# One core, attention block between two feed-forward halves: the last batch put first, head 0 staged from small writes, value groups moved behind

## The reference

```python
x = x + 0.5 * ffn(layernorm(x))          # layernorm again inside, 512 hidden, ternary weights, gelu, layernorm
x = x + attention(layernorm(x))
x = x + 0.5 * ffn(layernorm(x))
# attention, 16 heads of 8 channels
q = heads(x @ Wq + bq); k = heads(x @ Wk + bk); val = heads(x @ Wv + bv)
pos = (sinusoid(512, 128) @ Wp + bp) per head
score = (einsum(q + u, k) + relative_shift(einsum(q + v, pos))) / sqrt(8)
out = einsum(softmax(score), val) @ Wo + bo
```

## Time and profile before

| | |
|---|---|
| median of three runs | 447.42 us (446.59 to 447.7) |
| the profiled execution's own time | 447.46 us |
| its span, first to last instruction | 445.3 us |
| DVE busy over the span | 398.2 us (89%) |
| PE busy | 357.0 us (80%) |
| ACT busy | 263.9 us (59%) |
| POOL busy | 113.4 us (25%) |
| mean granted TensorE clock | 0.959 of full speed |

### The profile page before, as it was taken

How to read it: one execution, slowest core, us unless ns; L and a number is a source line. 1 busy time by engine, 2 the same in 40 slices (tenths; PEclk the granted TensorE clock), 3 DMA queues, 4 the chain that set the end, 5 groups by cost and what they waited for, 6 DMA issues and landing times.

```text
span 445.3 us, 18049 instructions
## 1 busy us (share of the span) xinstructions
PE 357.0 (80%) x7328; PEld 288.1 (65%) x7328; DVE 398.2 (89%) x579; ACT 263.9 (59%) x650; POOL 113.4 (25%) x157
## 2 busy tenths in 40 slices
PE   1869898756979889898898987988989889676974
PEld 1647675645767767677676766776767767573664
DVE  8786988429999999999999999999999999948685
ACT  1666555316666666666666666666666666614980
POOL 7543745390020201202102022020120210025552
PEclk9988899969899999999999999999999999988898
DMA  7005147920322313213133132231321301500002
GB/s 213 1 1 186 51 148 245 296 62 12 81 57 43 81 26 87 68 31 84 40 65 75 19 88 56 44 80 20 88 64 30 89 7 25 75 18 2 0 26 71
DMA packets 60182, 30.67 MB, mean 69 GB/s; under 512 B 36880, under 2 KB 58928, under 8 KB 60016
## 3 DMA queue, kind: packets, MB, share of 16 engines
q1 hardware_dynamic: 59376, 29.22, 25.8%
q10 hardware_dynamic: 576, 0.73, 0.6%
q0 software_dynamic: 192, 0.18, 0.2%
HBM read 19.11 MB, written 11.01 MB: 68 GB/s over the span
## 4 chain that ended last, share of the span: by engine, by line
DVE 58%; issue 17%; PE 11%; ACT 5%; POOL 2%; SPq 2%; DMA 2%; DVEq 1%; POOLq 0%; ACTq 0%
DVE pT L894 30%; DVE negmax L886 19%; PE pair L1014 3%; ACT v_rep L602 2%; DVE xh L702 2%; ACT v_rep L590 1%; PE pair L969 1%; DVE v_rep L820 1%; DVE sqsum L814 1%; DMA qs_scratch<-pT 1%; SPq L309 1%; PE pair L1183 1%; DMA stage_k<-kc_scratch 1%; DVE stat L692 1%; PE pair L1116 1%
## 5 line engine op out<-in xcount | busy, mean ns | idle before, releaser
L633 ACT ACTIVATE probs<-pair,negmax 128x512 f32<-128x512 f32 x256 | 173.7, 683 | 111.3 <-DVE negmax L886 111.3
L886 DVE TENSOR_REDUCE negmax<-pair 128x2 f32<-128x1024 f32 x128 | 152.1, 1188 | 10.4 <-PE pair L1133 10.4
L894 DVE STREAM_TRANSPOSE pT<-probs 128x1024 f32<-128x1024 f32 x128 | 157.0, 1226 | 0.5 <-ACT probs L633 0.5
L1116 PE MATMUL pair<-stage_k,stage_c 128*32 128x512 f16 x1024 | 117.2, 408 | 47.4 <-ACT probs L633 40.8
L1122 PE MATMUL pair<-stage_z,stage_q 128*32 128x512 f16 x1024 | 111.4, 384 | 0.0
L1133 PE MATMUL pair<-stage_z,stage_q 128*32 128x438 f16 (+58 forms) x1024 | 102.9, 282 | 0.0
L508 POOL COPY v_diag<-v_rep 32x512 f32 (+1 forms) x64 | 38.9, 607 | 233.9 <-PE pair L1148 226.5
L1128 PE MATMUL pair<-stage_z,stage_q 128*32 128x16 f16 (+50 forms) x1024 | 97.9, 277 | 0.0
L1148 PE MATMUL pair<-pT,v_diag 128*32 128x128 f32 (+1 forms) x2176 | 93.3, 271 | 3.6 <-DVE pT L894 3.6
L1116 PEld LDWEIGHTS pair<-stage_k,stage_c 128*32 128x32 f16 x1024 | 50.7, 140 | 69.5 <-ACT probs L633 55.4
L1148 PEld LDWEIGHTS pair<-pT,v_diag 128*32 128x32 f32 x2176 | 73.3, 114 | 4.1 <-DVE pT L894 3.8
(11 more groups left out here) (112 smaller groups left out, 326.0 us busy)
## 6 DMA issues: line engine op xcount, KB each, us to landing
stage_z<-z_scratch SPq DMA_DIRECT2D x16, 254.0 KB
qs_scratch<-pT SPq DMA_DIRECT2D x12, 256.0 KB, 2.7
stage_q<-qs_scratch SPq DMA_DIRECT2D x126, 24.0 KB
stage_z<-z_scratch SPq DMA_DIRECT2D x16, 128.0 KB
qc_scratch<-pT SPq DMA_DIRECT2D x8, 256.0 KB, 3.5
kc_scratch<-pT SPq DMA_DIRECT2D x8, 256.0 KB, 3.5
stage_k<-kc_scratch SPq DMA_DIRECT2D x16, 128.0 KB
stage_z<-z_scratch SPq DMA_DIRECT2D x16, 127.5 KB
```

The source lines that it names most:

```text
L633: nc.scalar.activation(probs[:, q % 6, :], score_pair(q // 2)[:, q % 2, :], ACT.Exp, bias=negmax[:, q % 8:q % 8 + 1], accum_out=rowsum[:, ...
L886: nc.vector.tensor_reduce(negmax[:, 2 * n % 8:2 * n % 8 + 2], score_pair(n)[:, :, :], AX.X, ALU.max, negate=True).then_inc(max_ready, 1)
L894: nc.vector.transpose(pT[:, par, 2 * n:2 * n + 2, :].rearrange("p a s -> p (a s)"), probs[:, 2 * n % 6:2 * n % 6 + 2, :].rearrange("p a s ...
L1116: mm(bank[32 * j:32 * j + 32, :], all_rows[:, 32 * j:32 * j + 32], stage_k[:, par, :], start=True, stop=False, skip_group_check=True)
```

## The change

Five things are edited.

1. **Order.** The last batch's moments move from step 20 to 18 and its statistics from 21 to 19, its tiles from 22 to 21, its turn from 23 to 22. The products of batch 2 move from step 22 to 23, directly ahead of batch 3's. The rounding of a batch's products stands ahead of the copy of `xT` in a step.
2. **Value groups.** No group goes with the first three batches. Twelve follow the last products on PE, and four (12 to 15) stand inside head 0, behind its score tiles 8, 10, 12 and 14. ACT copies those four behind the exponentials of tiles 9, 11, 13 and 15. ACT copies twelve of the 16 groups, DVE four.
3. **Writes.** Batch 3's data for head 0 go out in small writes: the first 16 channels of its queries (one DMA on SP, two on ACT), the first 8 of its content queries (two on SP). The rest of batch 3 and the keys of batch 2 are written by SP when head 0's own loads have landed (nine DMAs). Scratch layouts change so that a head's rows lie together.
4. **Head 0's loads.** Keys go from SBUF to SBUF without DRAM (`first_keys`, two DMAs a batch: on POOL for batches 0 to 2, on SP for batch 3). The eight query reads are split four and four between SP and POOL.
5. **Head 1's loads.** The eight query reads of head 1 move from SP to POOL, where they stand behind the spreading of head 0's values. PE waits for them with `staged_second`.

```diff
+MOMENT_STEPS = ({8: 0, 12: 1, 16: 2, 18: 3}, {8: 0, 12: 1, 16: 2, 20: 3})
+X_STEPS = ({9: 0, 13: 1, 17: 2, 19: 3}, {9: 0, 13: 1, 17: 2, 21: 3})
+XHAT1_STEPS = {12: 0, 16: 1, 20: 2, 21: 3}
+TURN1_STEPS = {14: 0, 18: 1, 21: 2, 22: 3}
+QK_STEPS = {17: 0, 20: 1, 23: 2, 24: 3}
...
-V_EARLY = 6
-LOADS_FIRST = 6
+V_HEAD = 12
+V_DVE = (5, 7, 9, 11)
+V_ACT = tuple(m for m in range(V_GROUPS) if m not in V_DVE)
+V_TILES = {8: 12, 10: 13, 12: 14, 14: 15}
...
+        def first_keys(eng, b, done):
+
+            c = slice(b * S, (b + 1) * S)
+            for a in range(2):
+                r = 32 * b + 16 * a
+                eng.dma_start(stage_k[r:r + 16, 0, :], rep_ap(half[0:HP, 2 + a, c], [(0, 2), (1, S)]))\
+                    .then_inc(done, 16)
...
# SP
+            sp.wait_ge(v_extended, 2 * B)
+            write_queries(sp, B - 1, 0, slice(0, EARLY), q_first)
+            sp.wait_ge(q_split, 2 * B)
+            write_content(sp, B - 1, 0, 1, u_first)
+            sp.wait_ge(k_split_last, 1)
+            first_keys(sp, B - 1, staged[0])
+            sp.wait_ge(q_out, 16 * 3 * (B - 1))
+            sp.wait_ge(q_first, 16 * 3)
             sp.wait_ge(stage_zero, 8)
-            stage_queries(sp, 0, 0, staged[0], range(NI - 2))
-            sp.wait_ge(k_out, 32 * B)
-            stage_keys(sp, 0, 0, staged[0])
+            stage_queries(sp, 0, 0, staged[0], range(4))
+            sp.wait_ge(u_first, 32)
+            stage_content(sp, 0, 0, B - 1, staged[0])
+
+            sp.wait_ge(staged[0], 16 * LOADS_EVEN)
+            sp.wait_ge(k_split, B - 1)
+            write_keys(sp, B - 2)
+            for kind in range(3):
+                write_queries(sp, B - 1, kind, slice(EARLY, D), q_out)
+            write_content(sp, B - 1, 1, H, u_out[B - 1])
+            write_keys(sp, B - 1)
 
             for b in range(B):
                 sp.wait_ge(u_out[b], 32)
                 stage_content(sp, 1, 1, b, staged[1])
+            sp.wait_ge(k_out, 32 * B)
             stage_keys(sp, 1, 1, staged[1])
-            stage_queries(sp, 1, 1, staged[1])
...
# POOL, behind ffn(0)
-            stage_queries(pool, 0, 0, staged_first, range(NI - 2, NI))
-            pool.wait_ge(u_out[B - 1], 32)
-            stage_content(pool, 0, 0, B - 1, staged_first)
+            pool.wait_ge(q_out, 16 * 3 * (B - 1))
+            pool.wait_ge(q_first, 16 * 3)
+            stage_queries(pool, 0, 0, staged_pool, range(4, NI))
...
             for par in range(2):
-                pool.wait_ge(v_copied[par], V_GROUPS // 2)
+                pool.wait_ge(v_copied[par], len((V_ACT, V_DVE)[par]))
             spread_v(0, 0)
+            pool.wait_ge(q_out, 16 * 3 * B)
+            stage_queries(pool, 1, 1, staged_second)
             spread_v(1, 1)
...
# ACT, in ffn(0) behind the rounding of batch 3, and in head 0
+                        if QK_STEPS[n - 1] == B - 1:
+                            act.wait_ge(q_high, 2 * B - 1)
+                            write_queries(act, B - 1, 1, slice(0, EARLY), q_first)
+                            act.wait_ge(v_extended, 2 * B - 1)
+                            write_queries(act, B - 1, 2, slice(0, EARLY), q_first)
...
+            for q in range(NQ):
+                exp_tile(0, q)
+                if q - 1 in V_TILES:
+                    copy_values(V_TILES[q - 1])
...
# PE
+                if m in (0, 2):
+
+                    pe.wait_ge(q_split, m + 4)
+                    pe.wait_ge(k_split, m // 2 + 2)
+                elif m >= 4:
+                    values_copied(pe, m - 2 if m >= V_HEAD else m - 4)
...
+                    if first and q in V_TILES:
+                        v_product(V_TILES[q])
...
-            pe.wait_ge(staged_first, 16 * LOADS_FIRST)
-            head(0, 0, 16 * (LOADS - LOADS_FIRST), True)
-            head(1, 1, 16 * LOADS)
+            pe.wait_ge(staged_pool, 16 * LOADS_POOL)
+            head(0, 0, 16 * LOADS_EVEN, True)
+            pe.wait_ge(staged_second, 16 * NI)
+            head(1, 1, 16 * LOADS_ODD)
```

More of the change, by code:

```diff
@@ L111, in macaron_kernel @@
         pTf = pT[:, :, :, :].rearrange("p a q s -> p (a q s)")
-        wq_sb, wk_sb, wv_sb, wp_sb = (pTf[:, 128 * n:128 * n + 128] for n in range(4))
+        wq_sb, wk_sb, wp_sb = (pTf[:, 128 * n:128 * n + 128] for n in (0, 1, 3))
+        wv_sb = wv[:, :]
         embT = pTf[:, 512:1024]
@@ L254, in v_bank, with values_copied @@
         def v_bank(n):
-            return 2 + n % 2 if n < V_EARLY else 2 + (n - V_EARLY) % 4
+            return 4 + n % 2 if n >= V_HEAD else 2 + n % 4
         def v_groups(step):
[L260 to L263, removed]
+            return range(V_HEAD) if QK_STEPS.get(step) == B - 1 else ()
+        def values_copied(eng, m):
+            by_dve = m in V_DVE
+            eng.wait_ge(v_copied[by_dve], (V_ACT, V_DVE)[by_dve].index(m) + 1)
         def score_pair(n):
@@ L309, in stage_queries, with write_queries, write_content, write_keys @@
                 eng.dma_start(dst, src).then_inc(done, 16)
+        def write_queries(eng, b, kind, r, done):
+            rows = (rep_ap(vl[r, b, :], [(NG, 2), (1, S)]), rep_ap(vh[r, b, :], [(0, 2), (1, S)]),
+                    rep_ap(vh[r, b, NG:], [(0, 2), (1, S)]))[kind]
+            eng.dma_start(qs_dram[r, :, kind, b * S:(b + 1) * S], rows).then_inc(done, 16)
+        def write_content(eng, b, h0, h1, done):
+            c = slice(b * S, (b + 1) * S)
+            for a in range(2):
+                eng.dma_start(qc_dram[h0:h1, b, a].rearrange("h p d n -> h (p d n)"), half[HP * h0:HP * h1, 0:2, c])\
+                    .then_inc(done, 16)
+        def write_keys(eng, b):
+            c = slice(b * S, (b + 1) * S)
+            for a in range(2):
+                eng.dma_start(kc_dram[:, b, a].rearrange("h p d n -> h (p d n)"),
+                              rep_ap(half[:, 2 + a, c], [(0, 2), (1, S)])).then_inc(k_out, 16)
         def rep_ap(view, dims):
@@ L338, in _ @@
             stage_pos(1, 1)
[L340 to L344, removed]
+            for b in range(B - 1):
+                sp.wait_ge(q_high, 2 * b + 1)
+                write_queries(sp, b, 1, slice(0, D), q_out)
+                sp.wait_ge(v_extended, 2 * b + 1)
+                write_queries(sp, b, 2, slice(0, D), q_out)
@@ L353, in _ @@
-                if b < B - 1:
+                write_content(sp, b, 0, H, u_out[b])
+                if b < B - 2:
                     sp.wait_ge(k_split, b + 1)
[L355 to L360, removed]
-            sp.wait_ge(stage_zero, 8)
@@ L465, in ffn @@
                             .then_inc(s["x_const"], 1)
-                    g = (n - 8) // 4
-                    if n % 4 == 0 and 0 <= g < B:
+                    g = MOMENT_STEPS[f].get(n)
+                    if g is not None:
                         r, v = grs[:, 4 * g:4 * g + 4], gvar[:, 4 * g:4 * g + 4]
@@ L642, in take_o @@
                 nc.scalar.activation(o_sb[:, par, :], ps[4 + par][:, 0:128], ACT.Copy).then_inc(o_ready, 1)
-            for h in range(2):
-                for q in range(NQ):
-                    exp_tile(h, q)
+            for q in range(NQ):
+                exp_tile(0, q)
+                if q - 1 in V_TILES:
+                    copy_values(V_TILES[q - 1])
+            for q in range(NQ):
+                exp_tile(1, q)
             for h in range(2, 4):
@@ L822, in ffn @@
                         nc.vector.tensor_tensor(sq_low, sqsum[:, :], sq_high, ALU.subtract).then_inc(s["sq_split"], 1)
-                    g = (n - 9) // 4
-                    if n % 4 == 1 and 0 <= g < B:
+                    g = X_STEPS[f].get(n)
+                    if g is not None:
                         dve.wait_ge(s["grstd"], g + 1)
@@ L876, in _ @@
             nc.vector.tensor_tensor(bo_row, bo_row, ps[6][:, 0:D], ALU.add).then_inc(bo_ready, 1)
-            for b in range(B):
-                dve.wait_ge(u_out[b], 32)
-            dve.wait_ge(k_out, 32 * B)
-            dve.wait_ge(q_out, 16 * 3 * B)
             def row_max(h, n):
@@ L891, in turn @@
                 dve.wait_ge(probs_ready, h * NQ + (2 * n + 2))
+                if n == 0 and isinstance(h, int) and h == 1:
+                    for b in range(B):
+                        dve.wait_ge(u_out[b], 32)
+                    dve.wait_ge(k_out, 32 * B)
+                    dve.wait_ge(q_out, 16 * 3 * B)
                 if n == 0 and not (isinstance(h, int) and h < 2):
```

104 lines of the change are left out of this document (52 added, 52 removed).

## The result

The changed kernel takes 454.42 us (median of 4 runs, 453.94 to 455.69), the kernel before 447.00 (4 runs, 446.01 to 447.70): ratio 1.0179, 95% interval 1.0141 to 1.0217. It is slower by 7.4 us; forecast were +3.6 and 451.0, with 447.2 to 455.8 as the range. So the direction and the place were right, and the change cost twice what was forecast. The profiled execution took 453.95 us, its span is 452.2 (before 445.3).

What follows compares the result with a forecast made beforehand. DVE's first turn, behind a DRAM staging path, was taken to bound the attention. Head 1's gap adds 13.6 us, the earlier first turn saves 10.0: +3.6 on 447.46 gives 451.0 us, range 447.2 to 455.8.

Steps and rivals of the forecast that it cites:

- The mechanism: Between heads 0 and 1: first turn 10.0 us earlier, then POOL's late reads idle PE and add 13.6 us.
- the staging path: Before head 0: SP's small writes from 75.4, four reads, one load landing at 85.1; PE starts at 85.8.
- the value groups in head 0: Inside head 0: four groups make PE's pair 2.5 us, hidden by PE running ahead; without cover 4 x 0.2 = 0.8.
- The feed-forward up to 56 us: Ahead of the edits: same order as before, so no change; batch 1's turn ends at 58.0.
- The clock stays at 2.4 GHz: Start of head 0: PE comes from twelve value groups without a gap; 4.1 us to the first turn, at 89.9.
- The third rival: Head 0 hardly earlier: staging ends at 88 to 89, half clock costs 2.2; 456.5, without the clock 453.5 to 454.3; 19%.
- The reads on POOL: Before head 1: eight query reads behind spreading head 0's values, 0.71 us apart, ends 0.57 and 0.85.
- Landing: Before head 1: the last query read lands 2.6 us after issue, 25.9 after the first turn; PE then starts.
- first maximum 2.91 of 2.87: Start of head 1: PE at half clock needs 2.87 us to the first maximum, 28.8 after the first turn.
- from batch 1's turn to the last products: Feed-forward's end: batch 1's turn ends at 58.0, last x at 62.5, 9.9 more to the last products at 72.4.
- The key loads that `xh` was to block: Rival: POOL's key loads wait for DVE's `xh` tiles, up to 1.1 us, 452.1; a quarter of the likeliest case's 53%.

Runs made afterwards that it cites:

- the first experiment: Changed kernel, but POOL issues head 1's eight query reads once the late writes have landed, ahead of the wait for copied values (reads first): 441.86 us, ratio 0.9908.
- the kernel with the dummies: Changed kernel plus four products with unused results on PE between the values and the wait for head 0's loads: 454.14 us, ratio 1.0200.

## Why the prediction had the place right and the size wrong

**The mechanism held.** Head 0 earlier, the reads on POOL only behind the last copy, PE idle for over ten microseconds, half clock at its start (0.50 in 116 to 120), DVE's longest wait at head 1's first maximum: each is in the trace, and the first experiment takes 12.6 us away with that one wait.

**The step that failed** is the staging path of head 0, forecast at 13.4 us and measured at 16.7, because SP's queue ahead of it was left out. With it and the clock behind PE's start (1.4, put at no loss) the first turn came 7.2 us earlier instead of 10.0; behind it the value groups in head 0 (1.9, put at nothing) come on top. Two came out lower than forecast and hide part of the miss: POOL's reads (-1.2), and one by luck, ahead of the edits (-2.7).

**The feed-forward up to 56 us, put at no change: -2.7, by luck.** Its order is the same, but not its clock. In the profile of before PE idles 2.42 us up to 30.72, and the windows show half clock:

```profile
30.72 0.18 PE L978 MATMUL pair<-mean,v_rep 128*128 128x1 f16 x1 [2.42 <-DVE v_rep L822]
```

```profile
30.00:32.00 2.00, 1.28 (x13) 1.28 (x14) 2.00 (x6) 1.31 (x3) 0.00 (x0) 0.50 0.00 0
34.00:36.00 2.00, 2.00 (x11) 2.00 (x11) 1.40 (x8) 0.30 (x1) 0.00 (x0) 0.50 0.62 235
```

After, the longer idle time comes earlier (2.18 us up to 23.30; only 1.27 there before), the clock falls in 24 to 26, and is back at 1.00 in 30 to 32. Batch 1's turn then ends at 55.28 instead of 58.01. All eight experiments show 1.00 in 30 to 32, and that turn starts at 53.5 to 54.4 in them (54.18 in the changed kernel, 56.91 before). Idle time alone does not explain it: the kernel with the reads first has the changed kernel's code up to here, idles as before did (1.27 us up to 23.49, 2.43 up to 30.52), and keeps the full clock from 18 to 46:

```profile
30.52 0.18 PE L1045 MATMUL pair<-mean,v_rep 128*128 128x1 f16 x1 [2.43 <-DVE v_rep L888]
```

```profile
30.00:32.00 2.00, 1.48 (x18) 1.36 (x19) 2.00 (x6) 1.10 (x2) 0.00 (x0) 1.00 0.03 8
```

So the clock takes different courses here in executions of the same code. None of the nine traces with the change loses these 2.7 us and the one trace of before does; whether the change earned them is not shown. For the forecast, which had no reason for them, they were luck: without them the two profiled executions differ by nearly 10 us, not 7.

**"The staging path", put at 13.4 us from the last products to PE's start: 16.7, so +3.3.** I counted the issues at 0.69 us, which is a read's pace, and let SP begin its small writes when the data is there. The pace was nearly right: the five small writes took 4.3 us for 3.45, the reads kept it (2.58 for four, 0.65 each), and PE started 2.2 us behind the issue of the last load, whose landing I had put at 3.5. What was wrong is where it begins. SP came to the small writes 7.4 us behind the last products (77.84), where I had 3.0, though POOL's piece for them was ready at 74.77. Ahead of them in SP's order stand the first seven of the chain, full writes of 256 KB, which took 8.5 us, 1.2 each; I had not counted them. In sum 4.4 and 0.9 more, 1.3 less, and 0.7 less that I had added on top of staging's 85.1: 3.3.

The experiments bear out that SP's queue sets the landing. The seven writes take 7.9 to 8.7 us in the six kernels that keep them, and in seven of the eight head 0's loads have landed 1.5 to 1.6 us behind the end of SP's chain, by SP's next write, which waits for them (3.0 with all value groups ahead). From the last products to that landing are 16.6 us in the changed kernel, 14.5 to 16.9 in those six, 13.5 and 14.6 in the two with batch 1's keys behind head 0's loads. So the forecast lies below all of these, the changed kernel near the upper end, and the late keys gain about 1.5 us, less than the scatter.

What stretches those writes is not settled. The view of waits puts 3.3 us of the seven on POOL's roundings and copies, but what batch 1's keys need of POOL had ended at 67.54, before their first write at 69.18, and what batch 2's queries need at 70.09; with the keys late that view has 0.2 us left, and the five writes that stay still take 1.2 each. The DMA engines, 0.90 busy, are not enough either: the kernel before issued its last seven writes of this size in 5.4 us, 0.8 each, with the engines fuller (1.05 in 78 to 82):

```profile
79.69 0.73 SPq L344 DMA_DIRECT2D qs_scratch<-pT  x1
...
82.08 1.98 SPq L351 DMA_DIRECT2D qc_scratch<-pT  x2
84.10 1.16 SPq L358 DMA_DIRECT2D kc_scratch<-pT  x2
```

**"The clock stays at 2.4 GHz", start to first turn 4.1 us: 5.54, so +1.4.** The start comes 3.63 us behind the value path, not at its end. With the clock held it is 4.4 (six kernels), so 1.1 of it is the clock. The third rival had named this loss, with staging at 88; half of that rival came true at 87.15.

**Value groups in head 0, put at 0, or 0.8 without cover: +1.9.** I compared PE's pair with DVE's pace and left out that the third group needs the first one's bank. Its copy stands on ACT behind a tile's exponential (100.93), PE waits 1.97, the clock drops to 0.77 in 100 to 104, and DVE waits 1.42 and 0.51. So the last exponential starts 16.51 us behind the first turn, not 14.35. With the copies early the waits go. By one more trace most of the loss is the clock and not the bank: in the kernel with the dummies PE waits longer for the same bank (2.45 us up to 101.00), the clock stays at 1.00 in 100 to 108, and DVE waits only 0.41:

```profile
102.79 1.23 DVE L947 TENSOR_REDUCE negmax<-pair 128x2 f32<-128x1024 f32 x1 [0.41 <-PE pair L1196]
```

**The reads on POOL, 0.71 apart: 0.54, so -1.2**, below the lower end that I gave (0.57). Landing 2.4 of 2.6 and first maximum 2.91 of 2.87 were right.

The rest: from batch 1's turn to the last products 15.2 of 14.4, +0.8. Together -2.7 + 0.8 + 3.3 + 1.4 = +2.8 at the first turn, and +0.7 in head 1 (1.9 and 0.3 on the way to the last exponential, -1.2, -0.2 for landing, and small terms): 3.5 on the forecast 3.6, which is the 7.1 of the trace. One sum of the prediction is off without consequence: in the third rival, staging at 88 without the clock's loss gives 453.3 (88 - 82.2 on 447.46), not 453.5.

The key loads that `xh` was to block lost little. POOL issues the first pair at 61.58, in 1.35 us, while DVE's four `xh` tiles run (61.92, 1.08 us); the second pair, at 67.83 with DVE idle, takes 1.20, the third 1.08 beside another operation of DVE (71.70):

```profile
61.58 1.35 POOL L321 DMA_DIRECT2D stage_k<-pT  x2 [0.32 <-POOL pT L536]
...
67.83 1.20 POOL L321 DMA_DIRECT2D stage_k<-pT  x2 [0.29 <-POOL pT L536]
```

The first pair took 0.15 to 0.27 us more than the others, and the slower of its two loads landed 4.2 us behind its issue, against 3.5 and 3.8. A wait for all four tiles, the rival's 1.1 us, is not there. The Trainium skill (SBUF — State Buffer, "SBUF: two separate sides") would have a DMA issued by POOL wait for such an operation if it runs in a 2-port mode. No run here shows the mode of the tiles, and a wait for the rest of one tile (0.27) is not excluded.

## What to carry to other kernels

When work is moved into a loop, follow its last piece to whatever waits for "all of it", and look at what is queued behind that waiter: here eight loads that needed none of it. Price a DMA issue from rows of the same kind under the same DMA load, and count the whole queue of the issuing engine ahead of it. A matmul engine that starts behind an idle stretch can have a second price besides the wait, and which stretch pays it can shift far from the edit: two single profiles may differ by some microseconds that no edit earned.

## What the runs showed of the hardware

- The granted clock fell behind idle times of PE of 3.63, 3.29 and 2.25 us ahead of head 0, and stayed at 1.00 behind 1.69, 1.64, 0.80 and 0.75. Start to first turn: 5.5 to 5.6 us against 4.4. The length alone does not decide: elsewhere it fell behind 2.42 us (up to 30.72, before) and held behind 2.43 (up to 30.52, reads first) and 2.45 (up to 101.00, dummies).
- Writes of 256 KB on SP's queue took 1.2 us each to issue between 69 and 78, with the DMA engines 0.90 busy, 0.8 in the kernel before with the engines fuller, and late writes of 224 to 256 KB 0.6 to 0.9 between 87 and 94; the 24 KB reads of head 0 took 0.65 in the changed kernel, 0.65 to 0.86 in the experiments. Two issues fewer ahead did not shorten the chain by their own length.
- POOL issues eight reads of 24 KB 0.54 us apart, in each of the nine kernels with the change.
